# Three score buffers, one bank of turned weights and one bank of outputs in a quantised cross-attention stage

## The chip, the cores and the metric

The kernel runs on one core of one Trainium2 chip. The metric is the device time of one execution in microseconds (us), the median of several runs. PE is TensorE, DVE is VectorE, ACT is ScalarE, POOL is GpSimd and SP is SyncE. PEld is the weight load of TensorE.

## The reference

The whole program is four pairs of a cross-attention and a feed-forward layer, each with its residual: `x = x + tanh(g) * layer(layernorm(x))`. x is 1024 tokens of 256 features (8 blocks of 128 tokens). The change is in the fifth of the eight layers alone, the attention of the third pair. Cut to what matters:

```
q = fq_sym((x @ Wq + bq) * hd**-0.5, axis=-1)   # 16 heads of 16
k, v = split(cond @ Wkv + bkv)                  # 1024 context rows
k = fq_sym(k, axis=-1);  v = fq_sym(v, axis=2)  # to 127 levels
attn = softmax(q @ k.T)                         # 1024 x 1024 for each head
attn = fq_unsigned(attn, axis=-1)               # to 255 levels of the row maximum
out = (attn @ v) @ Wp + bp
```

fq_sym and fq_unsigned round to multiples of a step that is the row's (for v the column's) largest value over 127 or 255.

## The kernel before

This stage first makes all keys (E_before_*), and then runs four steps (STEPS) of two token blocks each (G = 2; the code calls a block of the pair g). A step has 32 units (E_UNITS): unit u is head u // 2 of block u % 2, a 128 x 1024 piece of the scores. Everything is a software pipeline of slots, one a unit. In slot n each engine does, in the order of its stage list:

- PE: the extra piece of this slot if there is one, then scores(n) (2 matmuls of 512 columns, L2125), weigh(n-3) (8 matmuls of 16 columns, L2161), turn(n-2) (8 bf16 transposes of the rounded weights, L2145).
- DVE: reads, whole(n-2) (rounds the weights, L2275), extra, maximum(n) (row maximum of 128 x 1024 scores, L2265, and a small scaling, L2267).
- ACT: exps(n-2) (L2210), p_T(n-3) (copies the turned weights out of PSUM, L2203), then its extra copy.

The slots of a step run from 8 to 39, so that the tail of one step overlaps the head of the next. Five kinds of extra piece stand in fixed slots, each for block 0 in the even slot and block 1 in the next: E_X (slots 14 and 15, turn the next step's normed x, L2100), E_Q (16, 17, project q, L2106, read by DVE at L2240), E_STACK (30, 31, turn the stacked quantised q, L2112, copied by ACT at L2195), E_OT (36, 37, turn the outputs, L2179, copied by ACT at L2221), E_PROJ (38, 39, output projection, L2184, read by DVE at L2282 and added to x at L554). DVE scales the outputs of a step before that (L2298 to L2300), and quantises the next q in slots 19 and 22.

PSUM has 8 banks of 128 x 512 float32. `bank(g, n)` is bank 4g + n. Each block has four banks of its own: 0 for its 16 head outputs, 1 for the turned weights and for all of its extra pieces in turn, 2 and 3 for one unit's scores. So the waits of PE before are these:

```
scores(u): pe.wait_ge(E_exp.sem, E_exp.nth(i, u - G))
turn(u):   pe.wait_ge(E_pT.sem, E_pT.nth(i, u - G))
extra(n):  pe.wait_ge(E_pT.sem, E_pT.nth(i, n - 4))
```

turn also waits for the reader of the extra piece that stood before it in the bank (xT_ready, E_qread, E_qTs, E_oTs or E_outread). In every slot weigh(n-3) waits for the copy p_T(n-3), and it stands ahead of turn(n-2) in PE's order. In the last step slots 34 to 39 have no scores, and only the three first kinds of extra are left out.

Of the kernel before, what the change touches and what calls it, by code (L numbers as in the profile page):

```python
# [25 lines left out]
P = 128  # L26
# [3 lines left out]
G = 2  # L30
# [55 lines left out]
def program(nc, t, out, layers=8):  # L86

    with ExitStack() as ctx:
# [499 lines left out]
        B_q = flag("B_q")  # L588
# [1311 lines left out]
        E_o = flag("E_o")  # L1900
        E_oturned = flag("E_oturned")
# [12 lines left out]
        def E_before_tensor(pe, ch):  # L1914
# [21 lines left out]
            for b in range(NB + G):  # L1936
                if b < NB:
                    project_kv(b)
                if b >= G:
                    turn_kstack(b - G)  # L1940
                if b == 1:
                    for g in range(G):
                        E_turn_x(pe, 0, g)
                if b == 2:
                    for g in range(G):
                        E_project_q(pe, 0, g)
                if b in (4, 5):
                    E_turn_stack(pe, 0, b - 4)
            pe.wait_ge(E_kTs.sem, E_kTs.nth(0, NB - 1))

        def E_before_scalar(act, ch):
# [19 lines left out]
            for b in range(NB + G):  # L1971
# [6 lines left out]
                if b == 0:  # L1978
                    for g in range(G):
                        E_x_T(act, 0, g)  # L1980
                if b in (4, 5):
                    E_q_T(act, 0, b - 4)
# [7 lines left out]
        def E_before_vector(dve, ch):  # L1990
# [35 lines left out]
            for b in range(NB + G):  # L2026
# [11 lines left out]
                if b == 2:  # L2038
                    for g in range(G):
                        E_read_q(dve, 0, g)  # L2040
# [54 lines left out]
        head_of = lambda u: (u % E_UNITS) // G  # L2095

        def E_turn_x(pe, i, g):
            pe.wait_ge(xn_ready.sem, xn_ready.at(i, g))
            for k in range(KC):
                last = nc.tensor.transpose(bank(g, 1)[:, k * P:(k + 1) * P], xn[:, g, k * P:(k + 1) * P], ident[:])  # L2100
            last.then_inc(xnT_done.sem, 1)

        def E_project_q(pe, i, g):
            pe.wait_ge(xT_ready.sem, xT_ready.at(i, g))
            for k in range(KC):
                last = nc.tensor.matmul(bank(g, 1)[:, 0:D], xT[:, k, g, :], wE["q"][:, k, :], start=k == 0, stop=k == KC - 1)  # L2106
            last.then_inc(E_q.sem, 1)

        def E_turn_stack(pe, i, g):
            pe.wait_ge(E_qstack.sem, E_qstack.at(i, g))  # L2110
            for tt in range(TE):
                last = nc.tensor.transpose(bank(g, 1).bitcast(BF16)[:, tt * P:(tt + 1) * P],  # L2112
# [3 lines left out]
        def E_tensor(pe):  # L2116
            def scores(ch, i, u):
# [3 lines left out]
                if u >= G:  # L2121
                    pe.wait_ge(E_exp.sem, E_exp.nth(i, u - G))
                r = slice(ROWS * (h % 2), ROWS * (h % 2) + ROWS)
                for n in range(2):
                    last = nc.tensor.matmul(bank(g, 2 + n), E_[g]["qT"][r, h // 2, :], E_kT[r, h // 2, n * 512:(n + 1) * 512],  # L2125
# [3 lines left out]
            def turn(ch, i, u):  # L2129
                g = u % G  # L2130
                pe.wait_ge(E_pb.sem, E_pb.nth(i, u))
                if u >= G:
                    pe.wait_ge(E_pT.sem, E_pT.nth(i, u - G))
# [10 lines left out]
                for b in range(NB):  # L2144
                    last = nc.tensor.transpose(bank(g, 1).bitcast(BF16)[:, b * P:(b + 1) * P], E_[g]["pb"][:, b * P:(b + 1) * P], ident_b[:])  # L2145
                last.then_inc(E_pturned.sem, 1)

            def weigh(ch, i, u):
                h, g = head_of(u), u % G
                if u == 0:  # L2150
                    pe.wait_ge(prepared, PREPARED[4])
                    for b in range(NB):
                        last = nc.tensor.matmul(bank(1, 0)[:, D:2 * D], ones_b, E_vq[:, b, :], start=b == 0, stop=b == NB - 1)
                    last.then_inc(E_vsummed.sem, 1)
                if u == 1:
                    pe.wait_ge(E_vsummed.sem, E_vsummed.nth(0, 1))
                pe.wait_ge(E_pT.sem, E_pT.nth(i, u))
                if u >= E_UNITS and h == 0:
                    pe.wait_ge(E_o.sem, E_o.at(i, g))
                for b in range(NB):  # L2160
                    last = nc.tensor.matmul(bank(g, 0)[:, h * DE:(h + 1) * DE], E_[g]["pT"][:, b, :], E_vq[:, b, h * DE:(h + 1) * DE],  # L2161
# [3 lines left out]
            def extra(ch, i, n, what, g):  # L2165
                if what is None:
                    return
                if not (last_step(i) and n - 4 >= E_UNITS):
                    pe.wait_ge(E_pT.sem, E_pT.nth(i, n - 4))
                if what == E_X:  # L2170
                    E_turn_x(pe, i + 1, g)
                if what == E_Q:
                    E_project_q(pe, i + 1, g)
                if what == E_STACK:
                    E_turn_stack(pe, i + 1, g)
                if what == E_OT:
                    pe.wait_ge(E_o.sem, E_o.at(i, g))
                    for k in range(KC):
                        last = nc.tensor.transpose(bank(g, 1)[:, k * P:(k + 1) * P], E_[g]["t"][:, k * P:(k + 1) * P], ident[:])  # L2179
                    last.then_inc(E_oturned.sem, 1)  # L2180
                if what == E_PROJ:
                    pe.wait_ge(E_oTs.sem, E_oTs.at(i, g))
                    for k in range(KC):
                        last = nc.tensor.matmul(bank(g, 1)[:, 0:D], E_[g]["oT"][:, k, :], wE["p"][:, k, :], start=k == 0, stop=k == KC - 1)  # L2184
# [4 lines left out]
        def E_x_T(act, i, g):  # L2189
            act.wait_ge(xnT_done.sem, xnT_done.at(i, g))  # L2190
            nc.scalar.copy(xT[:, :, g, :], bank(g, 1)[:, 0:D].rearrange("p (k t) -> p k t", k=KC)).then_inc(xT_ready.sem, 1)

        def E_q_T(act, i, g):
            act.wait_ge(E_qturned.sem, E_qturned.at(i, g))
            nc.scalar.copy(E_[g]["qT"].rearrange("p a b -> p (a b)"), bank(g, 1).bitcast(BF16)).then_inc(E_qTs.sem, 1)  # L2195

        def E_scalar(act, ch):
            def p_T(ch, i, u):
# [4 lines left out]
                nc.scalar.copy(E_[g]["pT"].rearrange("p a b -> p (a b)").bitcast(F32), bank(g, 1)).then_inc(E_pT.sem, 1)  # L2203

            def exps(ch, i, u):
# [4 lines left out]
                nc.scalar.activation(E_[g]["e"], banks(g, 2), ACT.Exp, scale=small[:, g, h:h + 1],  # L2210
                                     bias=small[:, g, 48 + h:49 + h], accum_out=small[:, g, 64 + h:65 + h]).then_inc(E_exp.sem, 1)

            def extra(ch, i, n, what, g):
                if what == E_X:
                    E_x_T(act, i + 1, g)
                if what == E_STACK:
                    act.wait_ge(E_scores.sem, E_scores.nth(i, E_UNITS - G + g))
                    E_q_T(act, i + 1, g)
                if what == E_OT:
                    act.wait_ge(E_oturned.sem, E_oturned.at(i, g))  # L2220
                    nc.scalar.copy(E_[g]["oT"].rearrange("p a b -> p (a b)"), bank(g, 1)[:, 0:D]).then_inc(E_oTs.sem, 1)  # L2221
# [16 lines left out]
        def E_read_q(dve, i, g):  # L2238
            dve.wait_ge(E_q.sem, E_q.at(i, g))
            nc.vector.tensor_tensor(E_[g]["t"], bank(g, 1)[:, 0:D], E_bias[:, 0:D], ALU.add).then_inc(E_qread.sem, 1)  # L2240
# [18 lines left out]
        def E_vector(dve, ch):  # L2259
            def maximum(ch, i, u):  # L2260
# [4 lines left out]
                ch.link(nc.vector.tensor_reduce(small[:, g, 80:81], banks(g, 2), AX.X, ALU.max))  # L2265
# [13 lines left out]
            def reads(ch, i, n, what, g):  # L2279
                if what == E_PROJ:  # L2280
                    dve.wait_ge(E_out.sem, E_out.at(i, g))
                    nc.vector.tensor_tensor(E_[g]["u"], bank(g, 1)[:, 0:D], E_bias[:, 3 * D:4 * D], ALU.add).then_inc(E_outread.sem, 1)  # L2282
                    dve.wait_ge(E_outread.sem, E_outread.at(i, g))
                    add_to_x(dve, ch, i * G + g, E_[g]["u"], gates[:, 0, 2:3])
                if what == E_Q:
                    E_read_q(dve, i + 1, g)
# [718 lines left out]
```

## Time and profile before

| what | value |
|---|---|
| median of 3 runs | 1857.21 us (1846.9 to 1859.51) |
| profiled execution: its time | 1852.25 us |
| profiled execution: its span | 1850.5 us |
| mean granted TensorE clock | 0.808 of 2.4 GHz |
| busy over the span | PE 79%, DVE 66%, ACT 52%, POOL 13% |
| the stage's pipeline | from 1203 to 1549 us of the span |

The span is what the profiler records between the first and the last instruction; the profiled execution took 1.75 us more than that. Rows of the timeline begin with the start of an instruction (or of several like it merged) and how long it was busy, both in us. A bracket at the end is the time that the engine was idle before it, and whose work ended that.

### The profile page before, as it was taken

The numbers are of one execution on the slowest core, as the hardware profiler recorded it, in microseconds if no ns is written. First come the engines' busy times: TensorE is split into PE (matmuls) and PEld (weight loads), VectorE is DVE, ScalarE is ACT, GpSimd is POOL, SyncE is SP. The second block draws the span as 40 slices with busy tenths as digits, with TensorE's granted clock in tenths as the row PEclk, the third lists the DMA queues.
The fourth block names the chain that finished last, engine by engine and source line by source line (L and its number), as shares of the span: only waits on it lengthen the run. The fifth ranks groups of instructions, "written<-read, shape, count | busy, mean of one in ns | idle before, by whom it ended". The sixth has DMA issues, their size and how long they took to land.

```text
span 1850.5 us, 27056 instructions
## 1 busy us (share of the span) xinstructions
PE 1457.0 (79%) x9102; PEld 1021.9 (55%) x9122; DVE 1222.8 (66%) x2725; ACT 971.0 (52%) x2871; POOL 248.8 (13%) x323
## 2 busy tenths in 40 slices
PE   5774565288897988966999997488888898988786
PEld 4662443166665666655767764244444455766564
DVE  3676886679889898862342323589888896662432
ACT  2552766387787777842454441267667774312111
POOL 0000110144343443420000000000000000000000
PEclk7886867699999999996999998656656556987888
DMA  5202000100000000006000000000000001000000
GB/s 218 100 3 91 1 0 1 49 1 7 1 1 6 1 6 0 2 4 236 1 1 0 0 0 9 9 1 1 1 0 0 0 1 46 1 0 0 1 0 23
DMA packets 13574, 37.99 MB, mean 21 GB/s; under 512 B 2201, under 2 KB 8866, under 8 KB 10802
## 3 DMA queue, kind: packets, MB, share of 16 engines
q1 hardware_dynamic: 13490, 36.99, 5.2%
q8 instruction: 38, 0.62, 0.1%
q14 instruction: 46, 0.38, 0.1%
HBM read 35.94 MB, written 1.05 MB: 20 GB/s over the span
## 4 chain that ended last, share of the span: by engine, by line
PE 49%; DVE 32%; ACT 8%; issue 7%; POOL 1%; DMA 1%; DVEq 0%; ACTq 0%; SPq 0%; POOLq 0%; another core or an unknown queue 0%
PE PS L2145 4%; PE PS L2125 4%; PE PS L2757 4%; DVE small L2265 3%; DVE work L1116 2%; PE PS L1789 2%; PE PS L1745 2%; DVE work L2275 2%; PE PS L1734 2%; PE PS L1724 2%; PE PS L1769 2%; PE PS L1349 2%; PE PS L354 2%; PE PS L2792 2%; DVE small L1165 1%
## 5 line engine op out<-in xcount | busy, mean ns | idle before, releaser
L2265 DVE TENSOR_REDUCE small<-PS 128x1 f32<-128x1024 f32 x128 | 156.3, 1221 | 16.9 <-PE PS L2125 11.7
L2210 ACT ACTIVATE work<-PS,small 128x1024 f32<-128x1024 f32 x128 | 154.9, 1210 | 23.6 <-DVE small L2267 22.7
L206 POOL TENSOR_TENSOR rstd<-moments,eps 128x1 f32<-128x1 f32 x56 | 13.5, 240 | 1100.3 <-DVE moments L186 1100.3
L2145 PE MATMUL PS<-ident_b,work 128*128 128x128 bf16 x1024 | 122.9, 296 | 41.9 <-DVE work L2275 35.6
L1357 PE MATMUL PS<-late 128*128 128x512 f16 x384 | 101.4, 395 | 57.9 <-DVE work L1159 33.9
L1232 POOL TENSOR_TENSOR small<-small,minus_half 128x4 f32<-128x4 f32 x96 | 108.7, 1133 | 265.1 <-ACT small L1272 264.9
L2125 PE MATMUL PS<-early,work 64*128 64x512 bf16 x256 | 121.3, 572 | 4.4 <-ACT work L2210 2.8
L2145 PEld LDWEIGHTS PS<-ident_b,work 128*128 128x128 bf16 x1024 | 92.6, 133 | 47.2 <-DVE work L2275 36.1
L1322 ACT ACTIVATE work<-PS,small 128x128 f32<-128x128 f32 x256 | 90.2, 364 | 51.9 <-DVE small L1166 51.9
L2203 ACT COPY work<-PS 128x512 f32<-128x512 f32 x128 | 74.9, 585 | 66.7 <-PE PS L2145 66.7
L1357 PEld LDWEIGHTS PS<-late 128*128 128x128 f16 x384 | 35.8, 100 | 110.2 <-DVE work L1159 46.1
L2275 DVE TENSOR_SCALAR work<-work 128x1024 bf16<-128x1024 f32 x128 | 87.5, 684 | 7.1 <-ACT work L2210 5.0
L2161 PEld LDWEIGHTS PS<-work 128*128 128x128 bf16 x1024 | 37.0, 104 | 97.9 <-ACT work L2203 83.3
L1590 DVE TENSOR_TENSOR late<-late,PS 128x512 f32<-128x512 f32 x16 | 11.0, 687 | 117.1 <-ACT late L1650 117.1
L1288 ACT ACTIVATE work<-PS 128x128 f32<-128x128 f32 x256 | 67.0, 280 | 34.6 <-PE PS L1357 31.7
L1429 PE MATMUL PS<-work 128*128 128x128 f32 x512 | 75.5, 295 | 4.9 <-ACT work L1315 4.8
L1429 PEld LDWEIGHTS PS<-work 128*128 128x128 f32 x512 | 70.6, 209 | 13.8 <-ACT work L1315 10.5
L1243 POOL TENSOR_TENSOR work<-work 128x512 f16<-128x512 f32 x64 | 74.2, 1159 | 20.1 <-DVE work L1116 20.1
L1449 PE MATMUL PS<-work 128*128 128x256 f32 x256 | 66.6, 383 | 3.7 <-DVE work L1116 3.6
L2757 PE MATMUL PS<-work,late 128*128 128x256 f32 x256 | 66.2, 424 | 2.7 <-ACT work L2732 2.7
L1461 PE MATMUL PS<-late,work 128*128 128x256 f16 x480 | 64.9, 278 | 2.9 <-POOL work L1243 2.8
L1679 ACT ACTIVATE work<-PS,small 128x128 f32<-128x128 f32 x128 | 45.2, 365 | 37.7 <-DVE small L1600 37.7
(399 smaller groups left out, 3624.1 us busy)
## 6 DMA issues: line engine op xcount, KB each, us to landing
late<-in_C_proj SPq DMA_DIRECT2D x1, 4096.0 KB, 12.3
ctxT<-in_ctxT SPq DMA_DIRECT2D x24, 128.0 KB, 2.5
late<-in_C_q SPq DMA_DIRECT2D x1, 2048.0 KB, 8.8
late<-in_C_qx SPq DMA_DIRECT2D x1, 2048.0 KB, 13.1
late<-in_F_w SPq DMA_DIRECT2D x2, 1024.0 KB
late<-in_B_gate SPq DMA_DIRECT2D x1, 1024.0 KB, 9.1
late<-in_B_up SPq DMA_DIRECT2D x1, 1024.0 KB, 11.0
late<-in_B_down SPq DMA_DIRECT2D x1, 1024.0 KB, 13.4
```

The lines of the kernel that those rows point to most:

```text
L1232: return nc.gpsimd.tensor_tensor(rs, rs, minus_half[:, 0:4], ALU.pow)
L1243: nc.gpsimd.tensor_tensor(c["cat"], c["t"], c["m"], ALU.subtract).then_inc(C_cat.sem, 1)
L1322: last = nc.scalar.activation(C_[g]["p"][:, h, :], PS[:, SBANK, h * P:(h + 1) * P], ACT.Exp, scale=DC ** -0.5, bias=small[:, g, 8 + h:9 + ...
L1357: last = nc.tensor.matmul(PS[:, n, :], src(k), w, start=k == 0 and part == 0, stop=k == KC - 1 and part == 1)
L1429: last = nc.tensor.matmul(PS[:, SBANK, h * P:(h + 1) * P], c["qT"][:, h, :], c["kT"][:, 2 * (r % 2) + h // 2, :], start=True, stop=True)
L2125: last = nc.tensor.matmul(bank(g, 2 + n), E_[g]["qT"][r, h // 2, :], E_kT[r, h // 2, n * 512:(n + 1) * 512], start=True, stop=True)
L2145: last = nc.tensor.transpose(bank(g, 1).bitcast(BF16)[:, b * P:(b + 1) * P], E_[g]["pb"][:, b * P:(b + 1) * P], ident_b[:])
L2203: nc.scalar.copy(E_[g]["pT"].rearrange("p a b -> p (a b)").bitcast(F32), bank(g, 1)).then_inc(E_pT.sem, 1)
L2210: nc.scalar.activation(E_[g]["e"], banks(g, 2), ACT.Exp, scale=small[:, g, h:h + 1], bias=small[:, g, 48 + h:49 + h], accum_out=small[:, g ...
L2265: ch.link(nc.vector.tensor_reduce(small[:, g, 80:81], banks(g, 2), AX.X, ALU.max))
L2275: nc.vector.tensor_scalar(E_[g]["pb"], E_[g]["e"], MAGIC, MAGIC - 1.0, ALU.add, ALU.subtract).then_inc(E_pb.sem, 1)
L2757: last = nc.tensor.matmul(PS[:, bank_ + c % 2, n * D:(n + 1) * D], wH[name][:, k, at:at + P], H_rT[:, k, :], start=k == 0, stop=k == KC - 1)
```

## The change

The same matmuls, copies and vector operations are done. Other are the banks, some waits and some orders:

- Scores: unit u uses banks 0 and 1, 2 and 3, or 4 and 5, in turn. scores(u) waits for the exponential of the last user of that pair, mostly u-3. Where a step of 32 units wraps, `bank_used` gives u-2, u-5 or u-3.
- Bank 6 (E_T) takes the turned weights of both blocks and every extra piece. turn(u) waits for p_T(u-1), and extra(n) waits for p_T(n-3). The second E_OT waits for the copy of the first, the first E_PROJ for both copies, the second E_PROJ for the read of the first.
- Bank 7 (E_O) takes the outputs of both blocks. weigh of the next step waits until DVE has read both. DVE subtracts for both blocks in slot 35 (before: slots 34 and 35), and scales block 0 in slot 35 and block 1 in slot 36.
- The column sum of the values is read in DVE's slot 3 (before: 4), and weigh(0) waits for that (before: weigh(1)).
- DVE does whole(n-2) ahead of reads(n) (before: after it).
- In the stage that makes the keys the extra pieces keep their banks; the functions now take the bank as an argument.

```diff
+        E_oread = follow(B_q)
...
+        E_S = lambda u: 2 * ((u % E_UNITS) % 3)
+        E_T, E_O = PS[:, 6, :], PS[:, 7, :]
+        scores_of = lambda u: PS[:, E_S(u):E_S(u) + 2, :].rearrange("p a b -> p (a b)")
+
+        def bank_used(u):
+
+            v = u % E_UNITS
+            return u - (3 if v >= 3 else 5 if v == 2 else 2)
...
-                if u >= G:
-                    pe.wait_ge(E_exp.sem, E_exp.nth(i, u - G))
+                if bank_used(u) >= 0:
+                    pe.wait_ge(E_exp.sem, E_exp.nth(i, bank_used(u)))
...
-                if u >= G:
-                    pe.wait_ge(E_pT.sem, E_pT.nth(i, u - G))
+                if u:
+                    pe.wait_ge(E_pT.sem, E_pT.nth(i, u - 1))
...
                     last.then_inc(E_vsummed.sem, 1)
-                if u == 1:
                     pe.wait_ge(E_vsummed.sem, E_vsummed.nth(0, 1))
                 pe.wait_ge(E_pT.sem, E_pT.nth(i, u))
                 if u >= E_UNITS and h == 0:
-                    pe.wait_ge(E_o.sem, E_o.at(i, g))
+                    pe.wait_ge(E_oread.sem, E_oread.at(i, G - 1))
...
-                if not (last_step(i) and n - 4 >= E_UNITS):
-                    pe.wait_ge(E_pT.sem, E_pT.nth(i, n - 4))
+                pe.wait_ge(E_pT.sem, E_pT.nth(i, min(n - 3, E_UNITS - 1) if last_step(i) else n - 3))
...
                 if what == E_OT:
                     pe.wait_ge(E_o.sem, E_o.at(i, g))
+                    if g:
+                        pe.wait_ge(E_oTs.sem, E_oTs.at(i, g - 1))
...
                 if what == E_PROJ:
-                    pe.wait_ge(E_oTs.sem, E_oTs.at(i, g))
+                    pe.wait_ge(E_oTs.sem, E_oTs.at(i, G - 1))
+                    if g:
+                        pe.wait_ge(E_outread.sem, E_outread.at(i, g - 1))
...
-                if n == G + 2:
+                if n == G + 1:
                     dve.wait_ge(E_vsummed.sem, E_vsummed.nth(0, 0))
-                    nc.vector.tensor_copy(E_vsum, bank(1, 0)[:, D:2 * D]).then_inc(E_vsummed.sem, 1)
+                    nc.vector.tensor_copy(E_vsum, E_O[:, D:2 * D]).then_inc(E_vsummed.sem, 1)
 
             def extra(ch, i, n, what, g):
-                if n in (E_UNITS + 2, E_UNITS + 3):
-                    b = n - E_UNITS - 2
+                if n == E_UNITS + 3:
+                    dve.wait_ge(E_pv.sem, E_pv.at(i, G - 1, HE - 1))
+                    for b in range(G):
+                        nc.vector.tensor_tensor(E_[b]["t"], E_O[:, b * D:(b + 1) * D], E_vsum, ALU.subtract).then_inc(E_oread.sem, 1)
+                if n in (E_UNITS + 3, E_UNITS + 4):
+                    b = n - E_UNITS - 3
                     e = E_[b]
-                    dve.wait_ge(E_pv.sem, E_pv.at(i, b, HE - 1))
-                    ch.link(nc.vector.tensor_tensor(e["t"], bank(b, 0)[:, 0:D], E_vsum, ALU.subtract))
+                    dve.wait_ge(E_oread.sem, E_oread.at(i, b))
...
-            E_pipeline(dve, ch, lambda ch: None, [(None, reads), (2, whole), (None, extra), (0, maximum)])
+            E_pipeline(dve, ch, lambda ch: None, [(2, whole), (None, reads), (None, extra), (0, maximum)])
```

## Rows read from the trace of the kernel before

**Rows 1.** The page's part 1: busy time, share, instructions.

```profile
PE 1457.0 (79%) x9102; PEld 1021.9 (55%) x9122; DVE 1222.8 (66%) x2725; ACT 971.0 (52%) x2871; POOL 248.8 (13%) x323
```

**Rows 2.** Busy time by stretch: PE, PEld, DVE, ACT, POOL; clock, DMA.

```profile
1203.00:1549.00 346.00, 295.32 (x2444) 161.85 (x2444) 303.77 (x522) 243.00 (x406) 4.42 (x12) 0.58 0.00 1
...
1500.00:1536.00 36.00, 36.00 (x298) 18.44 (x297) 34.22 (x51) 29.82 (x52) 0.00 (x0) 0.50 0.00 1
1414.10:1424.70 10.60, 9.27 (x97) 5.36 (x94) 9.85 (x18) 8.68 (x16) 0.00 (x0) 0.98 0.00 0
```

**Rows 3.** Waits from 1203 to 1549: us in total, times, longest.

```profile
PEld PS L2125 <- ACT work L2210: 16.5, 63, 2.9
...
PE PS L2125 <- ACT work L2210: 2.8, 3, 2.0
```

**Rows 4.** Timeline of a plain slot at clock 0.50, all engines.

```profile
1274.52 1.03 PE L2125 MATMUL PS<-early,work 64*128 64x512 bf16 x2
...
1275.48 0.38 PE L2161 MATMUL PS<-work 128*128 128x16 bf16 x8
...
1275.59 1.23 DVE L2265 TENSOR_REDUCE small<-PS 128x1 f32<-128x1024 f32 x1
...
1275.72 1.01 PE L2145 MATMUL PS<-ident_b,work 128*128 128x128 bf16 x8
...
1276.67 1.03 PE L2125 MATMUL PS<-early,work 64*128 64x512 bf16 x2
1276.77 0.58 ACT L2203 COPY work<-PS 128x512 f32<-128x512 f32 x1 [0.36 <-PE PS L2145]
```

**Rows 5.** Timeline of a plain slot at full clock.

```profile
1250.20 1.22 DVE L2265 TENSOR_REDUCE small<-PS 128x1 f32<-128x1024 f32 x1
...
1250.42 0.62 PE L2145 MATMUL PS<-ident_b,work 128*128 128x128 bf16 x8 [0.37 <-DVE work L2275]
...
1251.07 0.58 ACT L2203 COPY work<-PS 128x512 f32<-128x512 f32 x1 [0.80 <-PE PS L2145]
...
1251.71 0.36 PE L2161 MATMUL PS<-work 128*128 128x16 bf16 x8
1252.18 1.22 DVE L2265 TENSOR_REDUCE small<-PS 128x1 f32<-128x1024 f32 x1
```

**Rows 6.** Timeline of slots 30 and 31 (E_STACK), second step.

```profile
1367.25 1.06 PE L2112 MATMUL PS<-ident_b,work 128*128 128x128 bf16 x8
1367.50 0.58 ACT L2203 COPY work<-PS 128x512 f32<-128x512 f32 x1 [0.36 <-PE PS L2145]
...
1371.35 1.06 PE L2112 MATMUL PS<-ident_b,work 128*128 128x128 bf16 x8
...
1371.59 0.59 ACT L2203 COPY work<-PS 128x512 f32<-128x512 f32 x1
```

**Rows 7.** Timeline of slots 13 to 18 (E_X, E_Q), third step.

```profile
1413.22 1.23 DVE L2265 TENSOR_REDUCE small<-PS 128x1 f32<-128x1024 f32 x1
...
1420.60 1.08 PE L2106 MATMUL PS<-late,xT 128*128 128x256 f32 x4
...
1424.64 1.22 DVE L2265 TENSOR_REDUCE small<-PS 128x1 f32<-128x1024 f32 x1
```

**Rows 8.** Timeline of slots 38 and 39 (E_PROJ), second step.

```profile
1391.63 2.02 PE L2184 MATMUL PS<-late,work 128*128 128x256 f32 x4
...
1398.56 1.22 DVE L2265 TENSOR_REDUCE small<-PS 128x1 f32<-128x1024 f32 x1
```

**Rows 9.** Timeline of the end of the stage, last step.

```profile
1542.27 0.42 DVE L2298 TENSOR_TENSOR work<-PS,work 128x256 f32<-128x256 f32 x1 [0.51 <-PE PS L2161]
...
1544.15 3.61 PE L2184 MATMUL PS<-late,work 128*128 128x256 f32 x8
...
1548.26 0.48 DVE L554 SCALAR_TENSOR_TENSOR X<-work,gates,X 128x256 f32<-128x256 f32 x1
```

**Rows 10.** Timeline of the beginning of the pipeline: maximum of slot 4.

```profile
1219.39 1.22 DVE L2265 TENSOR_REDUCE small<-PS 128x1 f32<-128x1024 f32 x1 [1.01 <-PE PS L2125]
```

More of the change, by code:

```diff
@@ L2144, in turn @@
                 for b in range(NB):
-                    last = nc.tensor.transpose(bank(g, 1).bitcast(BF16)[:, b * P:(b + 1) * P], E_[g]["pb"][:, b * P:(b + 1) * P], ident_b[:])
+                    last = nc.tensor.transpose(E_T.bitcast(BF16)[:, b * P:(b + 1) * P], E_[g]["pb"][:, b * P:(b + 1) * P], ident_b[:])
                 last.then_inc(E_pturned.sem, 1)
@@ L2152, in weigh @@
                     for b in range(NB):
-                        last = nc.tensor.matmul(bank(1, 0)[:, D:2 * D], ones_b, E_vq[:, b, :], start=b == 0, stop=b == NB - 1)
+                        last = nc.tensor.matmul(E_O[:, D:2 * D], ones_b, E_vq[:, b, :], start=b == 0, stop=b == NB - 1)
                     last.then_inc(E_vsummed.sem, 1)
-                if u == 1:
                     pe.wait_ge(E_vsummed.sem, E_vsummed.nth(0, 1))
@@ L2158, in weigh @@
                 if u >= E_UNITS and h == 0:
[L2159 removed]
+                    pe.wait_ge(E_oread.sem, E_oread.at(i, G - 1))
                 for b in range(NB):
[L2161 removed]
+                    last = nc.tensor.matmul(E_O[:, g * D + h * DE:g * D + (h + 1) * DE], E_[g]["pT"][:, b, :], E_vq[:, b, h * DE:(h + 1) * DE],
                                             start=b == 0, stop=b == NB - 1)
@@ L2180, in extra @@
                     last.then_inc(E_oturned.sem, 1)
                 if what == E_PROJ:
-                    pe.wait_ge(E_oTs.sem, E_oTs.at(i, g))
+                    pe.wait_ge(E_oTs.sem, E_oTs.at(i, G - 1))
+                    if g:
+                        pe.wait_ge(E_outread.sem, E_outread.at(i, g - 1))
                     for k in range(KC):
-                        last = nc.tensor.matmul(bank(g, 1)[:, 0:D], E_[g]["oT"][:, k, :], wE["p"][:, k, :], start=k == 0, stop=k == KC - 1)
+                        last = nc.tensor.matmul(E_T[:, 0:D], E_[g]["oT"][:, k, :], wE["p"][:, k, :], start=k == 0, stop=k == KC - 1)
@@ L2194, in E_q_T @@
+        def E_q_T(act, i, g, src):
             act.wait_ge(E_qturned.sem, E_qturned.at(i, g))
-            nc.scalar.copy(E_[g]["qT"].rearrange("p a b -> p (a b)"), bank(g, 1).bitcast(BF16)).then_inc(E_qTs.sem, 1)
+            nc.scalar.copy(E_[g]["qT"].rearrange("p a b -> p (a b)"), src.bitcast(BF16)).then_inc(E_qTs.sem, 1)
         def E_scalar(act, ch):
@@ L2202, in p_T @@
                     act.wait_ge(E_pv.sem, E_pv.nth(i, u - G))
-                nc.scalar.copy(E_[g]["pT"].rearrange("p a b -> p (a b)").bitcast(F32), bank(g, 1)).then_inc(E_pT.sem, 1)
+                nc.scalar.copy(E_[g]["pT"].rearrange("p a b -> p (a b)").bitcast(F32), E_T).then_inc(E_pT.sem, 1)
             def exps(ch, i, u):
```

59 lines of the change are left out of this document (29 added, 30 removed).

## The prediction, written before the change was run

> **What bounds the kernel now.** I read the page first for the shares: no engine is busy for all of the span, PE is the busiest with 79% [rows 1]. A share over eight layers says nothing about one of them, so next comes the table by stretch. The stage that is changed takes 346 us, with DVE busy for 303.77 us and PE for 295.32 us, at a granted clock of 0.58: most of it at 1.2 GHz [rows 2]. Then the timeline of single slots, since two engines so close together take turns.
>
> At 1.2 GHz a plain slot is PE's. From one scores to the next is 1276.67 - 1274.52 = 2.15 us: scores 0.96 to the start of weigh, weigh 0.24 to the start of turn, turn 0.95 to the next scores [rows 4]. No bracket stands on these rows, and from 1500 to 1536 us PE is busy for 36.00 of 36.00 us [rows 2]. At 2.4 GHz the slot is DVE's: maximum to maximum is 1252.18 - 1250.20 = 1.98 us, and PE idles 0.37 us before its turn [rows 5].
>
> The waits name what the change aims at. Scores wait for the exponential two units back: 16.5 us in 63 cases on the weight load, but only 2.8 us in 3 cases on the matmul [rows 3]. The first number is idle time of the weight loader alone, while the matmuls of turn were still streaming. So at most about 2.8 us can come from the third score buffer, and most of that is the fill of the pipeline.
>
> **The change, part by part.**
>
> *Third score buffer.* Worth 0 in a plain slot: at 1.2 GHz PE has no gap to fill, at 2.4 GHz DVE has none. Where DVE has a long extra (quantising the next q), PE is held by turn(n-2), which waits for rounded weights and stands behind scores in PE's order; another score buffer doesn't let it pass. I take 0, with 2.8 us as the most it can give [rows 3].
>
> *One bank for turned weights, plain slots.* turn(n-2) now waits for p_T(n-3). But weigh(n-3) stands just ahead of it in PE's queue and has waited for the same copy already. So 0.
>
> *One bank for turned weights, extra pieces.* This is where the change costs. extra(n) stands at the head of the slot, right behind turn(n-3), and now waits until ACT has copied exactly those weights out. Before it waited for n-4, long done. Queued behind it on PE are scores(n), weigh(n-3) and turn(n-2), and DVE's maximum(n) waits for scores(n). The price of one wait, from turn's start: the copy starts 1276.77 - 1275.72 = 1.05 us later, takes 0.58, and PE starts 0.06 us after a copy (1251.71 against 1251.07 + 0.58 = 1251.65), so 1.69 us; the piece used to start 0.95 us after turn's start. That is 0.74 us at 1.2 GHz [rows 4, 5]. At 2.4 GHz the copy starts 0.65 after turn's start, so 1.29 us in all; turn itself takes a little over half of 0.95, some 0.55 us with its gap: 0.74 again [rows 5]. The clock doesn't change it much, as most of it is ACT's copy.
>
> - E_STACK, slots 30 and 31. Before, the first piece starts at 1367.25 and the copy it would now wait for runs from 1367.50 to 1368.08: PE starts at 1368.14, +0.89. Everything behind it is a chain (scores, the copy of the stack, which waits for them, exponential, copy of the weights), so the second copy moves by as much, from 1371.59 to 1372.48; it ends 0.59 later and PE starts the second piece at 1373.13 in place of 1371.35: +1.78 in all [rows 6]. DVE idles for both in this stretch already, so nothing hides it. I take 1.8 a step.
> - E_X and E_Q, slots 14 to 17: four waits, 4 x 0.74 = 3.0 us. In the row's step this cluster has the full clock (0.98, [rows 2]) and DVE has 9.85 us of 10.60 busy, so PE has some slack that takes part of it. Walked slot by slot with the durations of rows 5 (copy of x and exponential between, ACT in order), the second E_Q starts at about 1423.2 instead of 1420.60 and the maximum of slot 18 at about 1426.8 instead of 1424.64, +2.2, against 11.42 us for the five slots before [rows 7]. At 1.2 GHz nothing is hidden: 3.0. I take 2.6 a step.
> - E_OT and E_PROJ, slots 36 to 39: four more waits, 3.0 us. Here the change gives something back. whole(n-2) no longer stands behind reads, so DVE rounds 0.6 us of weights in each of the two E_PROJ slots while it would have waited for the projection: -1.2. The scaling of the outputs is moved by a slot (three operations of some 0.42 us for each block, DVE's L2298 as in [rows 9]); weigh(32) waits for both subtractions, but turn(33) behind it isn't later than before, as DVE has the rounded weights ready sooner. That nets to 0. The joint wait of the first E_PROJ for both copies adds nothing, its copy of the weights comes later. So +1.8 where the clock rises with the projection; if it rises at the same time as before, when the first projection has run for 2.02 us mostly at 1.2 GHz (the later one would take about half, as 1.08 for an E_Q [rows 7]), the 1398.56 of slot 39 stays about where it is [rows 8]. Bounds 0 and 1.8, I take 1.0.
>
> *Beginning of the pipeline.* whole(0) now precedes the scaling of all values on DVE, so the first turn is done early; weigh(0) waits for the column sum to be read, which takes one copy of 0.42 us. The maximum of slot 4 waited 1.01 us for its scores, which stood behind the late turn [rows 10]. I take that gain: -1.0, bounds -1.0 and +0.5.
>
> *Tail of the last step.* No scores cover anything here. Before: second subtraction at 1542.27, both turns of outputs and both projections following with little between, the last addition over at 1548.74 [rows 9]. Now the chain is in series on one bank. From 1542.27: two subtractions 0.88, two products 0.92 to 1544.1; turn 0.7, copy 0.4 and hand-overs 0.15, then the same for the second block, to 1546.4; a projection of 3.61 / 2 = 1.8, read 0.45, the second projection 1.8, read and addition 0.95, with three hand-overs of 0.06: 1551.6. +2.9; I take 2.8.
>
> *Orders of SP and POOL* are not touched, and neither are DMAs.
>
> **Sum.** 3 steps x (1.8 + 2.6 + 1.0) = 16.2, + 2.8 for the tail, - 1.0 for the beginning: +18.0 us. The profiled execution took 1852.25 us, so it would take 1870. It lies 5 us under the median of the runs shown; on the median 1857.2 + 18.0 = 1875. With all low bounds: 3 x (1.8 + 2.2 + 0) + 2.8 - 1.0 - 2.8 = +11; with all high ones: 3 x (1.8 + 3.0 + 1.8) + 2.9 + 0.5 = +23.
>
> **The clock.** The 36 us in which PE has no gap at all ran at 0.50, and the E_X and E_Q cluster, with PE idle for 1.33 of 10.60 us, at 0.98 [rows 2]. So in this stage density alone does not bring the full clock, and the stretches that had it are the ones that the change takes apart. The Trainium skill, "TensorE: Matmul & The Clock Gate", Part 1, says that the throttle is the default and sustained matmul activity releases it; by that rule the gap-free stretch should have had the full clock, and here the trace does not agree. Its section on HAM oscillation says that pauses between bursts of matmuls bring the throttle back; by that the new waits cost grants, which is the second rival below.
>
> **Rivals.**
>
> 1. *The waits are covered* (the change costs next to nothing): if PE's new pause falls into time in which it would have waited for DVE anyway. For it: DVE is the busier engine of the stage [rows 2], at full clock PE idles 0.37 us a slot [rows 5]. Against: in E_STACK DVE itself idles, and at 1.2 GHz PE has no slack. It leaves the tail and half of the rest: +3 to +10, so 1860 to 1867.
> 2. *The clusters lose the full clock.* A slot chain there then pays turn, scores and projection twice as long: about 0.95 - 0.5 for each turn, as much for scores, and 1.0 for each projection. For E_X and E_Q that is 4 x 0.9 + 2 x 0.9 = 5.4 a step more, 16 in all: 1891.
> 3. *Faster: the stage gains the full clock.* If the third buffer or the new rhythm brings grants to plain slots, each falls from PE's 2.15 to DVE's 1.98, 0.17 us [rows 4, 5]. Some 90 of the 128 slots are plain ones at 1.2 GHz: at most 15 us. If the slots with extra pieces that now run at 1.2 GHz rise as well, the 0.9 us of a turn and a scores come off for each of 30: 27 us. Against the +18 of the waits this ends at 18 - 15 - 27 = -24, 1833. Place: plain slots first, where the trace shows PE at its densest and the clock at 0.50, which speaks against it; it decides from the point where the stage's mean clock is so far over 0.58 that half of those 42 us come back.
> 4. *It doesn't do what it says:* a wait names something already implied, so nothing moves. Only true for turn's wait, which I have at 0; it falls in with the first rival.
>
> **How the numbers follow.** Forecast 0.57, covered waits 0.20, lost clock 0.16, gained clock 0.07. 1% (about 18.6 us) is about what a measurement of this kernel tells from no change, and the forecast lies right at it: of its 0.57 I give 0.31 to over 1% and 0.26 to within. Slower by over 1%: 0.31 + 0.16 = 0.47; within 1%: 0.26 + 0.20 + 0.03 = 0.49; faster: 0.04. The range reaches from 1860, the low end of the first rival, to 1891, the second one's time.
>
> **What would show it.** Steps right: in the profile after, PE's first matmul of each extra piece carries an idle bracket with ACT's copy of the turned weights as releaser, 0.7 to 1.8 us; plain slots still take 2.15 us at 0.50 and 1.98 at full clock; the scores' wait for the exponential is gone; the 30 extra pieces outside the tail stand for about 16 us. The two E_STACK slots take together 1.8 us more. From the last subtraction to the last addition takes 2.8 us more. Wrong: plain slots get shorter; the pieces show no bracket; or the granted clock of the stage moves by more than 0.03, which would make the prediction wrong in either direction by more than any of its terms. So would a change of the clock in the layers behind, which keep their work but start at another time.

## The result and the profile after

The changed kernel takes 1887.23 us (median, 1884.33 to 1889.66), the kernel before 1854.99 us (1846.9 to 1859.51). The ratio is 1.018, with a 95% interval of 1.016 to 1.020: slower by 32 us, 1.6 to 2.0%. The forecast was 1875, in a range of 1860 to 1891.

The table by stretch, for the changed kernel: the stage's pipeline, then its three clusters of E_X and E_Q pieces (maximum of slot 13 to maximum of slot 18), then plain slots of the last step. Columns as in [rows 2].

```profile
1210.00:1589.00 379.00, 313.58 (x2444) 165.90 (x2444) 303.88 (x522) 243.21 (x406) 4.42 (x12) 0.54 0.00 1
...
1245.78:1264.89 19.11, 16.24 (x106) 8.48 (x105) 11.02 (x18) 9.66 (x18) 0.00 (x0) 0.50 0.00 1
1343.27:1360.84 17.57, 14.32 (x110) 7.78 (x109) 10.95 (x17) 9.76 (x18) 0.00 (x0) 0.63 0.00 0
1439.03:1456.52 17.49, 14.24 (x110) 7.78 (x109) 10.95 (x18) 9.77 (x18) 0.00 (x0) 0.63 0.00 0
...
1534.00:1572.00 38.00, 38.00 (x324) 20.05 (x324) 36.02 (x54) 31.45 (x54) 0.00 (x0) 0.50 0.00 1
```

The same three clusters in the kernel before:

```profile
1240.21:1252.18 11.97, 10.98 (x110) 6.68 (x109) 10.67 (x17) 9.55 (x18) 0.00 (x0) 0.85 0.00 0
1325.03:1338.61 13.58, 12.59 (x110) 7.54 (x109) 10.77 (x17) 9.66 (x18) 0.00 (x0) 0.72 0.00 0
1413.22:1424.64 11.42, 10.15 (x110) 6.24 (x109) 10.67 (x17) 9.44 (x18) 0.00 (x0) 0.94 0.00 0
```

DVE does the same 303.8 us of work [rows 2], in a stretch 33 us longer. The granted clock of that stretch is 0.54, where it was 0.58. The clusters grow by 4 to 7 us each, and their clock falls from between 0.72 and 0.94 to 0.50 and 0.63. The plain slots still have no gap on PE and the clock of 0.50.

The timeline of the changed kernel shows what the clusters are made of, here the first three pieces of the third step (slots 14 to 16):

```profile
1440.21 0.59 ACT L2214 COPY work<-PS 128x512 f32<-128x512 f32 x1 [0.36 <-PE PS L2154]
...
1440.94 0.69 PE L2109 MATMUL PS<-ident,xn 128*128 128x128 f32 x2 [0.77 <-ACT work L2214]
1441.56 1.03 PE L2134 MATMUL PS<-early,work 64*128 64x512 bf16 x2
...
1442.63 1.22 DVE L2276 TENSOR_REDUCE small<-PS 128x1 f32<-128x1024 f32 x1 [1.53 <-PE PS L2134]
...
1444.53 0.68 PE L2109 MATMUL PS<-ident,xn 128*128 128x128 f32 x2 [0.75 <-ACT work L2214]
...
1446.21 1.22 DVE L2276 TENSOR_REDUCE small<-PS 128x1 f32<-128x1024 f32 x1 [1.51 <-PE PS L2134]
...
1448.03 2.08 PE L2115 MATMUL PS<-late,xT 128*128 128x256 f32 x4 [0.68 <-ACT work L2214]
```

Each piece has a bracket, ended by the copy of the turned weights (L2214). In the 30 pieces of the three steps it is 0.67 to 0.77 us, and 0.86 in the second E_OT of each step. The piece is followed by scores, and DVE waits 1.5 us for these. Between the two E_X pieces lie 1444.53 - 1440.94 = 3.59 us. In the kernel before the same pieces carry no bracket.

A bracket is not yet the price of a wait. For that here are the turn and the E_X piece behind it, both at the clock of 0.50, first in the kernel before and then in the changed one:

```profile
1325.16 1.01 PE L2145 MATMUL PS<-ident_b,work 128*128 128x128 bf16 x8
1325.97 0.64 PE L2100 MATMUL PS<-ident,xn 128*128 128x128 f32 x2
```

```profile
1245.91 1.01 PE L2154 MATMUL PS<-ident_b,work 128*128 128x128 bf16 x8
...
1246.96 0.59 ACT L2214 COPY work<-PS 128x512 f32<-128x512 f32 x1 [0.36 <-PE PS L2154]
...
1247.69 0.69 PE L2109 MATMUL PS<-ident,xn 128*128 128x128 f32 x2 [0.77 <-ACT work L2214]
```

From the start of turn to the start of the piece it was 1325.97 - 1325.16 = 0.81 us, and it is 1247.69 - 1245.91 = 1.78 now: 0.97 more, with a bracket of only 0.77. The slot, maximum to maximum, grows by 1.03 us, from 2.57 to 3.60.

The table below is read from the starts of the 128 row maxima, which come in the same order in all kernels. "First maximum to last" is called the pipeline below, and what follows the last maximum the tail. Times in us; three numbers are the first three steps.

| stretch | before | before, second trace | changed |
|---|---|---|---|
| maximum 0 to 8 | 24.80 | 24.80 | 23.65 |
| X and Q, slots 13 to 18 | 11.97, 13.58, 11.42 | 11.95, 12.05, 13.67 | 19.11, 17.57, 17.49 |
| STACK, 29 to 32 | 8.95, 10.66, 10.67 | 8.92, 9.13, 10.68 | 12.38, 12.38, 12.39 |
| outputs, 32 to 40 | 25.22, 25.25, 23.68 | 25.20, 25.26, 23.77 | 27.31, 27.10, 26.77 |
| quantising and plain, 18 to 29 | 27.70, 27.71, 27.69 | 27.71, 27.70, 27.71 | 27.71, 27.72, 27.70 |
| first maximum to last | 331.66 | 330.93 | 361.64 |

The differences are -1.15, +17.20, +6.87 and +7.03, which is all of the pipeline's +29.98 but for rounding. The tail adds 16.05 - 12.66 = 3.4 us (from the last maximum to the end of the last addition). These are its rows in the changed kernel; two projections of 2.05 us stand in series, each behind a bracket:

```profile
1572.79 1.22 DVE L2276 TENSOR_REDUCE small<-PS 128x1 f32<-128x1024 f32 x1
...
1579.05 0.75 DVE L2308 TENSOR_TENSOR work<-PS,work 128x256 f32<-128x256 f32 x2 [2.35 <-PE PS L2169]
...
1583.17 2.05 PE L2195 MATMUL PS<-late,work 128*128 128x256 f32 x4 [0.55 <-ACT work L2232]
...
1585.82 2.04 PE L2195 MATMUL PS<-late,work 128*128 128x256 f32 x4 [0.61 <-DVE work L2293]
...
1588.36 0.48 DVE L554 SCALAR_TENSOR_TENSOR X<-work,gates,X 128x256 f32<-128x256 f32 x1
```

Together 33.4 us, against 32.2 between the medians.

### The profile page after: what moved, and what is told of

The parts are those of the page before. It is cut to its first block, busy times and chain, and to the rows that moved or that the text cites. A ratio compares the mean times of both kernels' runs of the same rounds, so it can differ in the third digit from the quotient of the medians.

```text
span 1887.9 us, 27090 instructions
## 1 busy us (share of the span) xinstructions
PE 1485.7 (79%) x9122; PEld 1029.3 (55%) x9122; DVE 1222.3 (65%) x2725; ACT 971.5 (51%) x2871; POOL 249.0 (13%) x323
## 4 chain that ended last, share of the span: by engine, by line
PE 52%; DVE 30%; ACT 9%; issue 7%; POOL 1%; DMA 1%; DVEq 0%; ACTq 0%; SPq 0%; POOLq 0%; another core or an unknown queue 0%
PE PS L2134 4%; PE PS L2154 4%; PE PS L2771 3%; DVE small L2276 2%; PE PS L1745 2%; DVE work L1116 2%; PE PS L1789 2%; PE PS L1807 2%; PE PS L1349 2%; PE PS L1769 2%; PE PS L1734 2%; PE PS L1724 2%; PE PS L2806 1%; PE PS L354 1%; DVE work L1181 1%
## 5 line engine op out<-in xcount | busy, mean ns | idle before, releaser
L1357 PE MATMUL PS<-late 128*128 128x512 f16 x384 | 101.9, 397 | 58.0 <-DVE work L1159 33.4
L2134 PE MATMUL PS<-early,work 64*128 64x512 bf16 x256 | 125.7, 596 | 1.4 <-ACT early L1969 1.1
L2214 ACT COPY work<-PS 128x512 f32<-128x512 f32 x128 | 74.9, 585 | 77.2 <-PE PS L2154 77.2
```

The costliest lines, as they stand in the source:

```text
L1357: last = nc.tensor.matmul(PS[:, n, :], src(k), w, start=k == 0 and part == 0, stop=k == KC - 1 and part == 1)
L2134: last = nc.tensor.matmul(PS[:, E_S(u) + n, :], E_[g]["qT"][r, h // 2, :], E_kT[r, h // 2, n * 512:(n + 1) * 512], start=True, stop=True)
```

## The experiments

The theory: an extra piece stands right behind a turn, and now waits until ACT has copied what that turn wrote. The rivals: the shared bank of outputs, or the shared bank in plain slots, is the cost; or the third score buffer does something either way; or it is the clock alone. Each ratio below is to the kernel before as it ran beside that experiment: 1859.03 us for own_bank, two_scores and behind, 1857.31 for turned_per_block, filled, order_only and own_last, 1854.76 for the others.

**before_again**, the kernel before once more for a second trace. Expected:

> The kernel before once more, for a second trace. If the 6.7 us by which the stage's pipeline began later in the changed kernel's trace are only spread, this trace begins it anywhere from 1200 to 1213 us; if they belong to the change, it begins within 1 us of 1204.4. The pipeline itself, first to last maximum, should be 331.7 us give or take 3.

1858.98 us. Its first maximum is at 1214.63 us, against 1204.42 in the first trace and 1211.15 in the changed kernel. That is even later than the 1200 to 1213 expected for mere spread. So the 6.7 us later start there needs no cause in the change, and it is why stretches are compared here and not positions. The pipeline took 330.93 us, and the X and Q clusters exchange their clocks (11.95, 12.05 and 13.67 us).

**own_bank.** Two score buffers, and the freed bank for all extra pieces. Their wait for the copy goes, and turn's wait for the piece's reader too; pieces wait for one another's readers.

```diff
-        E_S = lambda u: 2 * ((u % E_UNITS) % 3)
+        E_S = lambda u: 2 * ((u % E_UNITS) % 2)
-        E_T, E_O = PS[:, 6, :], PS[:, 7, :]
+        E_T, E_O, E_XB = PS[:, 6, :], PS[:, 7, :], PS[:, 5, :]
...
-                pe.wait_ge(E_pT.sem, E_pT.nth(i, min(n - 3, E_UNITS - 1) if last_step(i) else n - 3))
```

> The changed kernel, but with two score buffers and the freed bank given to all extra pieces. The turned weights of both blocks still share one bank, and the outputs share one. Theory (the extra pieces' wait for the copy of the turned weights costs the time): the wait is gone, so about all of the +32 us goes, 1848 to 1862 us; the X and Q cluster takes 11.5 to 14 us again, with the clock above 0.7 in it. Rival (the shared bank of outputs, or the shared bank for the turned weights in plain slots costs it): it stays at 1875 to 1890.

1847.62 us, ratio to before 0.993 (0.990 to 0.996). The whole is 11 us under the kernel before, and just under the expected range. The tail keeps its loss (15.94 us, against 12.66 before and 16.05 changed), so that loss is outweighed elsewhere. Clusters of X and Q: 10.72, 13.30 and 12.04 us, with a clock that is above 0.7 in two of them:

```profile
1244.91:1255.63 10.72, 9.94 (x110) 6.10 (x109) 10.50 (x18) 9.50 (x18) 0.00 (x0) 0.94 0.00 0
1326.32:1339.62 13.30, 12.82 (x110) 7.42 (x109) 10.77 (x17) 9.67 (x18) 0.00 (x0) 0.67 0.00 0
1410.90:1422.94 12.04, 11.56 (x110) 6.91 (x109) 10.75 (x17) 9.68 (x18) 0.00 (x0) 0.75 0.00 0
```

The turned weights still share one bank here, and so do the outputs: neither is the cost. Left are the extra pieces in the bank of the turned weights, and the third score buffer, which this kernel lacks too.

**two_scores.** The changed kernel with two score buffers.

```diff
-        E_S = lambda u: 2 * ((u % E_UNITS) % 3)
+        E_S = lambda u: 2 * ((u % E_UNITS) % 2)
...
-            v = u % E_UNITS
-            return u - (3 if v >= 3 else 5 if v == 2 else 2)
+            return u - 2
```

> The changed kernel with two score buffers instead of three, nothing else. Theory (the third score buffer is worth nothing, as PE has no gap at 1.2 GHz and DVE has none at 2.4): 1884 to 1891 us, within 3 us of the changed kernel. Rival (the third buffer does give something and the other parts cost more than 32 us): 1893 or more.

1889.23 us, ratio to before 1.016 (1.014 to 1.019); the pipeline took 361.71 us against 361.64. The third score buffer is worth nothing in this kernel, and the cost is the extra pieces in the shared bank.

**behind.** The changed kernel with the piece between weigh and turn.

```diff
-[(None, extra), (0, scores), (3, weigh), (2, turn)]
+[(0, scores), (3, weigh), (None, extra), (2, turn)]
```

> The changed kernel with the extra piece between weigh and turn in PE's order instead of ahead of scores. weigh has waited for the same copy, so the new wait costs nothing there; but turn now stands right behind the piece and waits for its reader (0.5 us for a copy of x or outputs, 1.1 for the stack), which scores used to cover. Theory (one bank with two hand-overs a slot is the cost, wherever the piece stands): the slot of an E_X falls from 3.6 to about 3.3 us, of an E_Q from 4.9 to 4.7, in all 5 to 12 us less: 1875 to 1882. Rival (only the place of the wait ahead of scores is to blame): nearly all comes back, under 1865.

1887.74 us, 1.015 (1.013 to 1.018). The expected 1875 to 1882 did not come, the total stayed the same. Of the single slots the second with an E_X takes 3.37 us and the last with an E_Q 4.74, as expected, but the slot between them, the first with an E_Q, takes 5.93, which the expectation had overlooked. The timeline of behind shows the pause in its other place:

```profile
1249.08 0.67 PE L2109 MATMUL PS<-ident,xn 128*128 128x128 f32 x2
1249.78 0.37 ACT L2202 COPY xT<-PS 128x256 f32<-128x256 f32 x1 [1.22 <-PE PS L2109]
...
1250.30 1.01 PE L2154 MATMUL PS<-ident_b,work 128*128 128x128 bf16 x8 [0.55 <-ACT xT L2202]
...
1252.44 0.67 PE L2109 MATMUL PS<-ident,xn 128*128 128x128 f32 x2
...
1255.81 2.05 PE L2115 MATMUL PS<-late,xT 128*128 128x256 f32 x4
...
1260.55 2.05 PE L2115 MATMUL PS<-late,xT 128*128 128x256 f32 x4
```

The clusters of X and Q are 18.36 us in all three steps, all at 0.50. That is 0.75 less than the changed kernel's 19.11 at the same clock, but the changed kernel has the higher clock for the end of its two others. STACK falls to 11.18, the outputs rise to 28.11, 28.09 and 26.61. A bank that weights and pieces share has two hand-overs to ACT or DVE in such a slot, and PE pays one of them wherever the piece stands. The rival, that only the place is to blame, falls.

**wait_alone** and **turned_per_block.** turned_per_block is the changed kernel with two score buffers and a bank for turned weights and pieces per block again, with the waits of before. What is left is the shared bank of outputs, the order on DVE and the earlier column sum. wait_alone puts back one line.

```diff
-                if not (last_step(i) and n - 4 >= E_UNITS):
-                    pe.wait_ge(E_pT.sem, E_pT.nth(i, n - 4))
+                pe.wait_ge(E_pT.sem, E_pT.nth(i, min(n - 3, E_UNITS - 1) if last_step(i) else n - 3))
```

> The changed kernel with two score buffers and a bank for turned weights and extra pieces per block again, with the waits of before. What is left of the change is the shared bank of outputs, the order of whole and reads, and the earlier column sum. Theory: those are worth the 1.2 us of the beginning and about 1 us in each step where the projections stand, so 2 to 6 us faster than before: 1852 to 1857. Rival (the shared bank of outputs costs, as weigh waits for both blocks): 1862 or more.

> turned_per_block with one wait changed: an extra piece waits for p_T(n-3), as in the changed kernel, though the bank that it uses has been free since p_T(n-4). Theory (this wait is the cost, and what else shares the bank adds only in the tail and where OT and PROJ stand in series): the X and Q clusters take 17 to 19 us with a clock of 0.50 to 0.65, the whole is 24 to 33 us slower than turned_per_block, 1878 to 1887. Rival (a good part of the loss is that turn of the other block waits for the reader of the piece, which one bank brings with it): under 15 us slower, below 1869.

turned_per_block: 1854.13 us, ratio to before 0.998 (0.996 to 1.000), pipeline 325.93 us, so the rest of the change is no loss. The shared bank of outputs costs nothing that shows in the whole; with the moved scaling it may have its part in the tail, which takes 13.78 us where it was 12.66. The outputs' stretch is 23.47, 23.46 and 23.00 us, under the kernel before in every step. wait_alone: 1885.01 us, 1.017 (1.015 to 1.019), pipeline 358.37 us, 32.4 more than without the line (tail 13.90). Its clusters of X and Q:

```profile
1240.10:1257.70 17.60, 14.35 (x110) 7.79 (x109) 10.95 (x18) 9.78 (x18) 0.00 (x0) 0.63 0.00 0
1335.87:1353.39 17.52, 14.27 (x110) 7.79 (x109) 10.96 (x18) 9.78 (x18) 0.00 (x0) 0.63 0.00 0
1431.48:1448.98 17.50, 14.25 (x110) 7.79 (x109) 10.95 (x17) 9.77 (x18) 0.00 (x0) 0.63 0.00 0
```

Its STACK stretches are 12.39, 12.39 and 12.40 us, as in the changed kernel, and the outputs take 27.10, 27.02 and 25.54 us. One wait, on a copy that the bank itself doesn't need, brings nearly all of the loss.

**filled.** two_scores with two float32 transposes of a constant into the free bank ahead of each wait; nobody reads them.

```diff
+                for _ in range(2):
+                    nc.tensor.transpose(PS[:, 4, 0:P], ident[:], ident[:])
                 pe.wait_ge(E_pT.sem, E_pT.nth(i, min(n - 3, E_UNITS - 1) if last_step(i) else n - 3))
```

> The changed kernel with two score buffers, and in each slot with an extra piece two float32 transposes of a constant into the free bank, whose result nobody reads, ahead of the wait for the copy: PE has something to do in the new pause of 0.77 us. Theory (the pauses keep the clock low in the clusters, and that is the part of the loss beyond the waits): the granted clock of the three X and Q clusters rises from 0.50 to 0.63 to over 0.75, they take 14 to 16 us in place of 17.5 to 19.1, and the whole is 6 to 14 us faster than two_scores, 1875 to 1883. Rival (the clock follows something else, the waits alone cost): the same clusters within 1 us and the whole within 4 us, or slower by up to 5 us where the fill runs past the pause.

1886.72 us, 1.018 (1.013 to 1.023). The clusters:

```profile
1236.51:1252.82 16.31, 14.13 (x118) 8.03 (x118) 10.95 (x18) 9.73 (x18) 0.00 (x0) 0.75 0.00 1
1332.18:1351.29 19.11, 17.95 (x113) 9.65 (x113) 11.04 (x17) 9.67 (x18) 0.00 (x0) 0.50 0.00 0
1429.61:1447.16 17.55, 15.81 (x118) 8.88 (x118) 10.95 (x17) 9.77 (x18) 0.00 (x0) 0.63 0.00 0
```

One rose to 0.75 and took 16.31 us, one fell back to 0.50, one stayed. The whole is the same within its interval. The fill did not close the pause: at the clock of 0.50 the E_X and E_Q pieces keep brackets of 0.25 to 0.34 us. But the cluster in which PE is idle least, 1.16 of 19.11 us, is the one that stays at 0.50. So keeping PE busy with this work does not reliably bring the clock back, and my theory of how the clock was lost is not borne out. No other work than transposes was tried as a fill.

**order_only.** The kernel before with whole ahead of reads on DVE.

```diff
-[(None, reads), (2, whole), (None, extra), (0, maximum)]
+[(2, whole), (None, reads), (None, extra), (0, maximum)]
```

> The kernel before with whole ahead of reads on DVE, nothing else. Theory: PE's next turn no longer waits for the read of the projection, the two slots of E_PROJ get 0.3 to 0.6 us shorter each, and the pipeline begins sooner: 2 to 5 us in all, 1853 to 1857. Rival (the reads came first for a reason, they free the bank that turn waits for): same or up to 4 us slower.

1854.02 us, 0.999 (0.997 to 1.001). In its trace the pipeline is 326.91 us, 4.0 to 4.8 shorter than in the two of before; the whole lies in the expected range, but can't be told from the kernel before.

**own_last.** own_bank with the piece last in PE's slot and DVE's maximum ahead of reads and extra.

```diff
-[(None, extra), (0, scores), (3, weigh), (2, turn)]
+[(0, scores), (3, weigh), (2, turn), (None, extra)]
...
-[(2, whole), (None, reads), (None, extra), (0, maximum)]
+[(2, whole), (0, maximum), (None, reads), (None, extra)]
```

> own_bank with the extra piece last in PE's slot, and DVE's reads and extra work after its maximum. An extra piece then holds up neither the scores nor the turned weights of its own slot. Theory: where the piece comes first it delays scores by its own 0.4 to 2 us, which DVE feels at 1.2 GHz; 4 to 10 us faster than own_bank, 1838 to 1844. Rival (ACT's and DVE's waits for the later piece hold up their next exponential and maximum by as much): within 3 us of own_bank or slower.

1902.89 us, 1.026 (1.022 to 1.031): not faster but over 50 us slower than own_bank, so the rival holds. Waits of own_last, columns as in [rows 3]:

```profile
PE PS L2133 <- ACT work L2218: 35.8, 19, 2.3
DVE work L2283 <- ACT work L2218: 35.8, 20, 2.8
```

ACT waits for the late piece ahead of its next exponential, and scores and the rounding of weights wait 35.8 us each for that. Here, with the exponential late, the second score buffer is short; a third might have had something to do; that wasn't tried.

**own_two_turned.** own_bank with banks 4 and 6 for the turned weights of the two blocks.

```diff
+        E_Tg = (PS[:, 4, :], PS[:, 6, :])
...
-                if u:
-                    pe.wait_ge(E_pT.sem, E_pT.nth(i, u - 1))
+                if u >= G:
+                    pe.wait_ge(E_pT.sem, E_pT.nth(i, u - G))
```

> own_bank with two banks for turned weights, one per block, so that all eight banks are used. Theory (weigh has waited for the same copy already, so one bank for turned weights costs nothing where nothing else is in it): within 3 us of own_bank, 1844 to 1851. Rival (the single bank does hold turn up somewhere): 4 us or more faster than own_bank.

1849.19 us, 0.996 (0.993 to 1.000). As far as the two intervals tell, one bank for turned weights costs nothing once no extra piece is in it. The trace has a use of its own, as its clusters stay at 1.2 GHz for long. Here is the third one:

```profile
1411.65:1425.06 13.41, 12.93 (x110) 7.43 (x109) 10.77 (x18) 9.67 (x18) 0.00 (x0) 0.66 0.00 0
```

Its slots take 2.57, 2.57 and 3.96 us at 0.50, then 2.32 and 1.98 at full clock. In wait_alone's third cluster the first three are at 0.50 as well and take 3.60, 3.59 and 4.90; the next has 0.88 and takes 3.43, the last 1.99 at full clock. So at nearly the same clock four waits cost 17.50 - 13.41 = 4.1 us, 1.0 each. The two kernels differ in more than that wait; but turned_per_block, which differs from wait_alone in nothing else, says the same with its second cluster, 13.23 us at 0.68 against 17.52 us at 0.63.

**own_stack_late.** own_bank with ACT's copy of the stack behind the next slot's exponential.

```diff
+            def stack(ch, i, n, what, g):
+                if n - 1 in (E_STACK, E_STACK + 1) and not last_step(i):
+                    b = n - 1 - E_STACK
+                    act.wait_ge(E_scores.sem, E_scores.nth(i, E_UNITS - G + b))
+                    E_q_T(act, i + 1, b, E_XB)
...
-            E_pipeline(act, ch, lambda ch: None, [(2, exps), (3, p_T), (None, extra)])
+            E_pipeline(act, ch, lambda ch: None, [(2, exps), (None, stack), (3, p_T), (None, extra)])
```

> own_bank with ACT's copy of the stacked q moved behind the exponential of the next slot. ACT waits 1.3 us for the last scores ahead of that copy while an exponential is ready. Theory: the three slots around E_STACK fall from 9.1 to 9.6 us to about 8.5, so 2 to 4 us faster than own_bank, 1843 to 1846. Rival (PE's scores of the next step wait for that copy, which now comes later): same or slower.

1844.92 us, 0.995 (0.993 to 0.997). STACK falls to 8.04, 8.89 and 8.89 us, from 9.56, 9.12 and 9.56 in own_bank. In its timeline the exponential (L2218) now runs ahead of the copy (L2203), which finds its scores done:

```profile
1370.28 1.21 ACT L2218 ACTIVATE work<-PS,small 128x1024 f32<-128x1024 f32 x1
...
1371.69 1.01 ACT L2203 COPY work<-PS 128x1024 bf16<-128x1024 bf16 x1
```

The gain of 2.4 us in STACK is smaller than the spread of the whole, and own_bank and own_stack_late can't be told apart: their intervals overlap. Both beat both kernels of the study.

## Why the prediction was right, and where it was too small

The way and the mechanism were forecast, and the time lies in the range. The size was not: 32 us came for 18. Three steps of the working were too small, and these are the price of one wait, the clock of the clusters and the low bound of the outputs.

*Third score buffer, 0:* right, two_scores shows it. The bracket rule held: the 16.5 us of [rows 3] stood on the weight load alone, and were no time to be gained.

*Plain slots, 0:* right. The stretches without pieces are equal to 0.03 us, and own_two_turned agrees, where the turned weights get their second bank back.

*Extra pieces, the mechanism:* right. Every piece has the forecast bracket, and wait_alone brings the loss with that wait alone.

*The price of one wait, 0.74:* mis-sized, it is 1.0 us. The working let the piece start 0.95 us after turn's start. But that is the distance from turn to scores in a plain slot [rows 4]; from turn to a piece it was 0.81 us. It also let PE start 0.06 us after the copy, but from the copy's end to the piece 1247.69 - (1246.96 + 0.59) = 0.14 us pass. That the brackets of 0.67 to 0.77 us look like the 0.74 of the working is chance: a bracket counts from the end of turn and not from where the piece used to start.

*E_STACK, 1.8 a step:* right where the clock is the same. It was worked out from the rows of the pieces themselves and not from the 0.74. The slots grew by 0.86 and 0.86 us in the second and third step (3.00 to 3.86, 4.09 to 4.95), 1.72 in all against 1.78. In the first step it was 3.43, as there the kernel before had the higher clock.

*E_X and E_Q, 2.6 a step:* this term of the sum was mis-sized, and most of the error is here: 17.20 us came for 7.8. Two things are in it. The waits cost 4.1 us a step at nearly the same clock (wait_alone against own_two_turned), over the upper bound of 3.0, and nothing of them was hidden; no run has all four at full clock, where the working had 2.2. That makes 3 x 4.1 = 12.3 of the 17.2 (an estimate). The rest, some 5 us, is the clock, less what DVE's new order gives back. The working had two bounds for two clocks, but both left the clock itself as it was, and the 0.98 of [rows 2] is the best stretch of the best of the three clusters: over whole clusters the kernel before had 0.85, 0.72 and 0.94. The changed kernel had 0.50, 0.63 and 0.63. This is the mechanism of the second rival, at a third of the 16 us that it had for these pieces; part of it belonged in the forecast.

*E_OT and E_PROJ, 1.0 a step:* also mis-sized, 7.03 us came for 3.0, over the upper bound of 1.8 a step. The experiments take the term apart. What the new order gives back did come: turned_per_block is 1.75, 1.79 and 0.68 us under the kernel before in this stretch, 4.2 in all against the 3.6 of the working. The waits cost 3.6, 3.6 and 2.5 us (wait_alone over turned_per_block), against 3.0 each. The rest of the shared bank adds 0.2, 0.1 and 1.2 us. What failed is the low bound of 0, which pulled the term down to 1.0. In two steps the clock rose where that bound has it, with 2.07 us for the first projection and 1.13 for the second, and the stretch still grew by 2.1 and 1.9 us; in the third it rose later, and both projections took 2.1.

*Beginning, -1.0:* -1.15. *Tail, +2.8:* +3.4, as the projections took 2.05 instead of 1.8 us each.

*The range and the chances:* 1887 lies in the range only because this reached to 1891, the time of the lost clock. That end stood for 16 us of clock on top of the forecast; what came was some 5 of clock in those clusters, and waits and outputs too small in the sum. So that the range held was partly luck. "Slower by over 1%" had 0.47. And one sign of being wrong was met: the granted clock of the stage moved by 0.04, from 0.58 to 0.54, where the working allowed 0.03. A second sign failed too: the 30 pieces outside the tail stand for 31 us (17.20, 6.87 and 7.03) and not for 16. The others came out. The row of PE's matmul waiting for the exponential (L2125 in [rows 3]) has no successor in the changed kernel, and on the weight load 12.3 us in 60 cases of the 16.5 are left.

*The clock:* the gap-free plain slots stayed at 0.50, again for 38.00 us of 38.00 in the changed kernel, so the trace still speaks against the Trainium skill's rule in "TensorE: Matmul & The Clock Gate", Part 1, as the whole story. Its section on HAM oscillation, that pauses between bursts bring the throttle back, agrees in direction with 0.72 to 0.94 becoming 0.50 to 0.63. Over all kernels run, the 15 clusters with a pause at the pieces (of the changed kernel, two_scores, filled, behind and wait_alone) have 0.50 to 0.75, and the 21 of the seven traces without one (two of before, and turned_per_block, order_only and the own_ kernels but own_last) have 0.65 to 0.94. (own_last, whose waits stand elsewhere, has 0.61 to 0.62.) A part of this is only length: the waits stretch the part of a cluster that runs at 1.2 GHz, and that lowers the mean. In the second step turned_per_block has 0.68 over 13.23 us and wait_alone 0.63 over 17.52 us, and both make about 4.7 us at full clock. But a part is real: all 21 clusters without the pause end at full clock, and 6 of the 15 with it stay at 0.50 throughout. That the wait takes some of the clock along is so shown; how much of it is chance is not, as the kernel before alone goes from 0.72 to 0.94. Why the clock is lost, and what would hold it, stays open.

## What to carry to other kernels

Before merging buffers, look for the odd user that stands directly behind the common one in the queue: the bank was free for the steady work, and cost 32 us through 34 small pieces. A bracket on the weight load alone is no gain to be had; ask for one on the matmul. Work out the price of a new wait from the rows of the very instruction that will wait, from start to start: the plain slot gave 0.74 us here, the slot of the piece 1.0. And where a term lies in a stretch at full clock, price the loss of that clock in the forecast itself.

## What the runs showed of the hardware that was not expected

In plain slots PE was busy for 38.00 of 38.00 us at a granted clock of 0.50, while the clusters with float32 pieces and with PE idle for 0.99 to 1.27 us of 11 to 14 had 0.72 to 0.94. Slots 18 to 25 repeat to 0.04 us from run to run and kernel to kernel (19.10 to 19.14 us in every kernel but own_last), while the same code's clusters differ by 2 us with the clock they happen to get (11.42 to 13.67).
